# Graph recommender kernel: edges sorted into buckets that follow one another without padding, and a ring of 72 gathered tiles read through registers

## The reference: what is computed

```python
h = emb; acc = emb
for _ in range(2):
    h = jax.ops.segment_sum(adj_val[:, None] * h[adj_col], adj_row, num_segments=N)
    acc = acc + h
graph_item_embs = acc / 3
combined = graph_item_embs[items] + item_features[items]
seq_hidden = jnp.take_along_axis(combined, alias_inputs[..., None], axis=1)
... # masked mean, tanh, sigmoid gate, weighted sum over a session
item_out = _l2norm(graph_item_embs)      # scores = session vectors x all nodes
```

## Time and profile before

| what | value |
|---|---|
| median of 3 runs | 4148.01 us |
| the profiled execution | 4146.78 us, span 4145.0 us |
| mean granted TensorE clock | 0.755 of full |
| POOL busy | 2890.5 us (70%) |
| DVE busy | 3058.7 us (74%) |
| PE busy | 3105.1 us (75%) |
| layer 0, first to last gather | 742.7 to 2238.7 us |
| layer 1, first to last gather | 2265.7 to 3761.7 us |

### The profile page before, as it was taken

One profiled execution on the slowest core, in us unless ns is written; L12 is line 12 of the kernel. 1 busy time (PEld: TensorE's weight loads), 2 busy tenths in 40 slices (PEclk: granted clock), 3 DMA queues, 4 the chain that ended last, 5 costly groups with the idle time before them and its releaser, 6 DMA issues.

```text
span 4145.0 us, 77740 instructions
## 1 busy us (share of the span) xinstructions
PE 3105.1 (75%) x14462; PEld 2477.2 (60%) x14462; DVE 3058.7 (74%) x7236; ACT 824.8 (20%) x2833; POOL 2890.5 (70%) x2966
## 2 busy tenths in 40 slices
PE   4899998577777777777775777777777777776798
PEld 2777776466665666656664666666656665563454
DVE  8999997677777777777775676777767777677575
ACT  0899999000000000000000000000000000004553
POOL 2466766777777777777775777777777777775770
PEclk8899998676767777777766676777777777775898
DMA  1000000222222222222233222222222222233143
GB/s 36 3 4 3 3 3 3 57 55 55 55 55 55 55 55 55 55 55 55 55 100 119 56 56 55 55 56 55 56 55 56 55 55 56 55 116 102 58 155 144
DMA packets 156580, 236.68 MB, mean 57 GB/s; under 512 B 67566, under 2 KB 108216, under 8 KB 156184
## 3 DMA queue, kind: packets, MB, share of 16 engines
q0 software_dynamic: 92896, 171.14, 15.4%
q1 hardware_dynamic: 48364, 59.22, 4.2%
q10 hardware_dynamic: 15052, 3.83, 0.6%
HBM read 192.69 MB, written 41.33 MB: 56 GB/s over the span
## 4 chain that ended last, share of the span: by engine, by line
POOL 50%; issue 22%; DVE 10%; PE 9%; DMA 6%; ACT 2%; SPq 0%; DVEq 0%; ACTq 0%; POOLq 0%
POOL ring L577 48%; DMA ring<-in_L_rec_emb,cring 3%; PE bank L1479 2%; DMA ring<-table,cring 2%; PE bank L1420 2%; ACT big L647 2%; POOL ring L600 2%; DVE stage L926 1%; DVE big L870 1%; PE bank L1507 1%; DVE big L886 1%; DVE ring L1101 1%; DVE ring L878 1%; PE bank L1365 1%; PE bank L1466 1%
## 5 line engine op out<-in xcount | busy, mean ns | idle before, releaser
L1420 PE MATMUL bank<-ring 128*128 128x128 f32 x9952 | 2199.2, 381 | 816.2 <-DVE ring L1101 784.3
L1420 PEld LDWEIGHTS bank<-ring 128*128 128x128 f32 x9952 | 1831.2, 270 | 1184.0 <-DVE ring L1101 1158.4
L1101 DVE TENSOR_SCALAR ring<-bank,mlo,mval 128x256 f32<-128x256 f32 x2488 | 1349.2, 542 | 734.8 <-DMA ring<-table,cring 385.8
L577 POOL DMA_INDIRECT ring<-table,cring x1195 | 1132.4, 948 | 390.5 <-issue 355.9
L577 POOL DMA_INDIRECT ring<-in_L_rec_emb,cring x1195 | 1132.5, 948 | 368.8 <-issue 355.7
L1151 DVE TENSOR_TENSOR acc<-acc,bank 128x256 f32 x2488 | 1025.0, 412 | 142.5 <-issue 138.5
L663 ACT COPY mlo<-ring 128x24 f32 (+1 forms) x104 | 22.0, 211 | 2882.2 <-PE bank L1420 2793.3
L647 ACT ACTIVATE big<-big 128x68 f32<-128x68 bf16 x1764 | 557.3, 405 | 0.0
L1365 PE MATMUL bank<-big,ring 128*128 128x136 f32 x2352 | 441.5, 325 | 60.5 <-DVE ring L878 15.9
L545 POOL DMA_INDIRECT sorted_edges<-moved,block_to x313 | 399.9, 1278 | 101.7 <-issue 101.7
L1365 PEld LDWEIGHTS bank<-big,ring 128*128 128x128 f32 x2352 | 349.1, 212 | 150.9 <-ACT big L647 130.3
(11 more groups left out here) (210 smaller groups left out, 1438.7 us busy)
## 6 DMA issues: line engine op xcount, KB each, us to landing
ring<-in_L_rec_emb SPq DMA_DIRECT2D x3136, 0.5 KB
ring<-in_L_rec_emb ACTq DMA_DIRECT2D x3136, 0.5 KB
ring<-table SPq DMA_DIRECT2D x3136, 0.5 KB
ring<-table ACTq DMA_DIRECT2D x3136, 0.5 KB
scores<-stage SPq DMA_DIRECT2D x48, 512.0 KB, 2.7
ring<-in_L_rec_emb,cring POOLq DMA_INDIRECT x1195, 3.6
ring<-table,cring POOLq DMA_INDIRECT x1195, 3.5
table<-acc SPq DMA_DIRECT2D x7, 896.0 KB, 9.9
```

The costliest lines, as they stand in the source:

```text
L577: pool.indirect_dma_start(msg[:, s, :], None, source, bass.IndirectOffsetOnAxis(cring[:, s:s + 1], 0)).then_inc(s_g[s], 16)
L1101: dve.tensor_scalar(onehot[:, u % SR, :], bank[7][:, 0:BUCKET], mlo[:, u:u + 1], mval[:, u:u + 1], ALU.is_equal, ALU.mult).then_inc(s_S[u ...
L1420: last = pe.matmul(bank[u % PR][:, q * D:(q + 1) * D], onehot[:, u % SR, q * P:(q + 1) * P], msg[:, h * T + u, :], start=True, stop=True)
```

## The change

The bucket totals are no longer padded to tiles: a bucket starts where the one before ends (at a multiple of 4). That leaves GT = 1194 tiles of 128 slots per layer, but a tile may now hold edges of two buckets. The unit of the products becomes a *pass*: one tile and one bucket. There are 1194 + 48 passes, rounded up to 1244, so the number of products, `onehot` and adds is what the number of tiles was. A tile that crosses a border is gathered once and multiplied twice, each time with the values of the other bucket's edges set to zero.

- **Maps.** After the sort DVE computes for each bucket its first tile and first pass, PE turns these into per-pass tables (12 matmuls of 416 columns), and DVE derives which slots are valid in a pass, `pick` (a matrix that copies a tile's column to its passes), `slot_off` (the ring slot of a pass's tile, in elements) and `upto` (the group of gathers that a group of four passes needs). `m_lo` and `m_val` come from products with `pick` in place of transposes. The three matmuls for `tile_off` move from before the sort to after it.
- **Ring.** `msg` has RING = 72 slots in place of 48. PE reads the slot through a register; it loads 24 slot offsets and 6 group numbers per step.
- **Hand-over.** DVE no longer waits for gathers. POOL issues them in groups of four tiles; before group g it waits until group g - 2 has landed (for a group with an own tile, until its 128 one-row DMAs have, too) and raises `s_gd`; PE waits for `s_gd` against a register every four passes.
- **Pacing.** POOL's waits for products come only from tile 72 on: before tile 4g (g even) pass 4g - 16 must be done.
- **Own tiles.** 48 instead of 49 per layer, so POOL issues 1146 gathers per layer; the rows of own tile r start when the passes up to 24r are done (r = 1 and 2 need no wait on SP).
- The gather reads its indices from `m_col` directly; `cring` and its copy are gone.

```diff
+    GT = -(-(E + GR * NB * (R - 1)) // P)
+    NU = GT + NB - 1
-    NOWN = NST - 3
+    NOWN = GST - 2
+    RING = 3 * T
+    BEHIND = RING - (NB - 1)
+    GRP4 = 4
...
@@ sync
+            def own_tile(layer, source, r, h):
+                if not (isinstance(r, int) and r < 3):
+                    sp.wait_ge(s_mm[M - 1], r * (T // M) + PER * layer)
+                own_rows(source, r * HALF - HALF, h)
...
@@ gpsimd
+            def group_landed(layer, gi):
+                c, q = divmod(gi, T // GRP4)
+                pool.wait_ge(s_g[q], landed_of(layer, gi))
+                if is_own(T * c + GRP4 * q + GRP4 - 1):
+                    pool.wait_ge(s_line[c % 3], 16 * P)
+                    pool.sem_clear(s_line[c % 3])
+                pool.sem_inc(s_gd, 1)
+            def gather_group(layer, source, gi):
+                if gi >= 2:
+                    group_landed(layer, gi - 2)
+                if gi % 2 == 0 and GRP4 * gi >= RING:
+                    pool.wait_ge(s_mm[M - 1], PER * layer + (GRP4 * gi + 2 * GRP4 - BEHIND) // M)
+                for j in range(GRP4 * gi, min(GRP4 * gi + GRP4, GT)):
+                    if is_own(j):
                         continue
-                    if u % PACE == 0:
-                        done = NU * layer + T * c + u - AHEAD
-                        if done > 0:
-                            pool.wait_ge(s_mm[(done - 1) % M], (done - 1) // M + 1)
-                    pool.indirect_dma_start(msg[:, s, :], None, source,
-                                            bass.IndirectOffsetOnAxis(cring[:, s:s + 1], 0)).then_inc(s_g[s], 16)
+                    pool.indirect_dma_start(msg[:, j % RING, :], None, source,
+                                            bass.IndirectOffsetOnAxis(m_col[:, j:j + 1], 0)).then_inc(s_g[gi % (T // GRP4)], 16)
...
+                for gi in range(NGRP):
+                    if layer == 0 and gi == T // GRP4:
+                        pool.wait_ge(s_mrdy, 3)
+                    gather_group(layer, source, gi)
...
@@ scalar
-            act.wait_ge(s_toff, 3)
+            act.wait_ge(s_lcc, 1)
...
+            def round_rows(layer, source, r, k):
+                fetch(layer, r + 1, (k + 1) % 2)
+                own_rows(source, r * HALF - HALF, k % 3)
...
@@ vector
-            link(dve.tensor_scalar(toti[:, :], tot[:, :], float(P - 1), None, ALU.add))
-            link(dve.tensor_single_scalar(toti2[:, :], toti[:, :], P.bit_length() - 1, ALU.arith_shift_right))
-            link(dve.tensor_copy(ntile[:, :], toti2[:, :]))
...
-                if u % T < T - 1:
-                    dve.wait_ge(s_g[u], 16 * (FED[u] * layer + it + 1))
...
+                if u % T == 0:
+                    dve.wait_ge(s_mr, it * 2 + (NST * layer + u // T + 1))
...
@@ tensor
+                _, offs = nc.values_load_multi_w_load_instructions(
+                    slot_off[:, bass.ds(c * T, T)], engines=[mybir.EngineType.PE],
+                    min_val=0, max_val=(RING - 1) * D, skip_runtime_bounds_check_because=HERE)
+                _, need = nc.values_load_multi_w_load_instructions(
+                    upto[:, bass.ds(c * (T // M) + PER * layer, n // M)], engines=[mybir.EngineType.PE],
+                    min_val=1, max_val=LAYERS * NGRP)
+                for u in range(n):
+                    if u % M == 0:
+                        pe.wait_ge(s_gd, need[u // M])
                     pe.wait_ge(s_S[u % M], it * (2 * T // M) + (PER * layer + (T * h + u) // M + 1))
                     for q in range(2):
                         last = pe.matmul(bank[u % PR][:, q * D:(q + 1) * D], onehot[:, u % SR, q * P:(q + 1) * P],
-                                         msg[:, h * T + u, :], start=True, stop=True)
+                                         msg_flat[:, bass.ds(offs[u], D)], start=True, stop=True)
```

More of the change, by code:

```diff
@@ L110, in is_own, with landed_of @@
         return j % T == T - 1 and 1 <= j // T <= NOWN
-    FED = [sum(1 for j in range(u, NU, 2 * T) if not is_own(j)) for u in range(2 * T)]
-    assert T % 4 == 0 and max(TC[n + 1] - TC[n] for n in range(3)) <= 512
+    def landed_of(layer, gi):
+        c, q = divmod(gi, T // GRP4)
+        whole = [16 * sum(1 for k in range(GST) for j in range(T * k + GRP4 * q, min(T * k + GRP4 * q + GRP4, GT)) if not is_own(j))]
+        return layer * whole[0] + 16 * sum(1 for k in range(c + 1) for j in range(T * k + GRP4 * q, min(T * k + GRP4 * q + GRP4, GT))
+                                           if not is_own(j))
+    assert T % 4 == 0 and NP % 3 == 0 and NP // 3 <= 512 and NP - P * (NP // P) > 0 and P + NB - 1 <= 2 * P
+    HERE = "a pass's tile has its rows in one of RING slots: 0 to RING - 1, times D"
     with ExitStack() as ctx:
@@ L368, in recommender_program @@
         s_sid = sem("s_sid")
[L369 removed]
+        s_sq = [sem(f"s_sq{u}") for u in range(2 * NG)]
         s_x = sem("s_x")
@@ L448, in own_tiles @@
                     sp.wait_ge(s_t1w, 16 * (NB // GRP))
[L449 to L453, removed]
+                for r in range(1, 3):
+                    own_tile(layer, source, r, r)
+                with sp.Fori(1, NOWN // 3) as i:
+                    for h in range(3):
+                        own_tile(layer, source, 3 * i + h, h)
+                own_tile(layer, source, NOWN, 0)
             sp.wait_ge(s_mrdy, 3)
@@ new lines, in _ @@
+            some = plan[:, 4, :]
+            link(dve.tensor_copy(toti[:, :], start[:, :]))
+            link(dve.tensor_single_scalar(toti2[:, :], toti[:, :], P.bit_length() - 1, ALU.arith_shift_right))
+            link(dve.tensor_copy(ft, toti2[:, :]))
+            link(dve.tensor_scalar(toti[:, :], cum[:, :], float(P - 1), None, ALU.add))
+            link(dve.tensor_single_scalar(toti2[:, :], toti[:, :], P.bit_length() - 1, ALU.arith_shift_right))
+            link(dve.tensor_copy(le, toti2[:, :]))
@@ new lines, in _ @@
+            link(dve.tensor_tensor(le, le, ft, ALU.subtract))
+            link(dve.scalar_tensor_tensor(some, tot[:, :], 0.0, le, ALU.is_gt, ALU.mult))
+            link(dve.tensor_tensor_scan(begin, ones[:, 0:NB], some, 0.0, ALU.mult, ALU.add))
+            link(dve.tensor_tensor(begin, begin, some, ALU.subtract))
+            link(dve.tensor_tensor(shift, ft, begin, ALU.subtract))
+            dve.tensor_copy(bound[:, 2, :], shift)
+            link(dve.scalar_tensor_tensor(bound[:, 0, :], shift, -float(P), start[:, :], ALU.mult, ALU.add))
@@ new lines, in _ @@
+            link(dve.tensor_scalar(upto[:, 0:PER], upto[:, 0:PER], 1.0, None, ALU.add))
+            for n in range(3):
+                a, b = PC[n], PC[n + 1]
+                dve.wait_ge(s_map, n + 10)
+                last = dve.tensor_scalar(tile_off[0:1, a:b], bank[(3, 5, 6)[n]][0:1, 0:b - a], -1.0, float(BUCKET),
+                                         ALU.add, ALU.mult)
+            last.then_inc(s_slot, 1)
+            low_rows(0, 1, P).then_inc(s_low, 1)
+            for m in range(1, -(-NT // P)):
+                code_columns(m).then_inc(s_mtc, 1)
@@ new lines, in pass_chunk @@
+                last.then_inc(s_chk, 1)
+            pe.wait_ge(s_mapv, 9)
+            pe.wait_ge(s_meta0, 16)
+            turned(0)
+            pe.wait_ge(s_slot, 1)
+            pe.wait_ge(s_low, 1)
+            pass_chunk(0)
+            pe.wait_ge(s_meta, 32)
+            for m in range(1, -(-NT // P)):
+                turned(m)
+            pe.wait_ge(s_low, 3)
+            for m in range(1, -(-NP // P)):
+                pass_chunk(m)
+            pe.wait_ge(s_mta, -(-NP // P))
+            pe.wait_ge(s_pv, -(-NP // P))
```

286 lines of the change are left out of this document (185 added, 101 removed).

## The result

The changed kernel takes 4203.33 us (median of four runs, 4193.92 to 4204.8), the kernel before 4149.44 in the same set: a ratio of 1.013 (95% interval 1.0118 to 1.0143). The forecast was 4064 us, range 4028 to 4112, faster. It was wrong in sign and size.

A forecast was written before the change was run, and what follows sets the result against it. POOL's issue of gathers, 1.25 us each, was taken as the bound. Fewer gathers (-122.5) and smaller savings, less costs for landings, own rows, head and ends, summed to -83.3 us: 4064 us, range 4028 to 4112.

The forecast's parts named there:

- the wait for landed gathers: POOL's wait for group g-2: median landings cost nothing, only the late tail costs; +6 us over both layers, bounds 0 and 100.
- C: Rival: landing tails stop POOL in most steps, or later own-row rounds lose too; 52 us more, 4116 us; chance 0.13.
- forecast -122.5: Gathers on POOL: 1146 in place of 1195 a layer at 1.25 us each, -122.5 us over both layers.
- First gather: Start of layer 0's gathers: no wait for ACT's copy of `cring`, -0.8 us; start expected 2 us sooner, about 741.
- The head: First 24 gathers of layer 0: 7.5 us lost beside DVE operations, 4.3 before, and +1 us waiting for `m_col`.
- the 6 us more: Head of layer 0: if each DVE operation blocks POOL in full, about 6 us more, 4070 us in all.
- Own rows: POOL's wait for own tiles' row DMAs, mainly rounds 2 to 4: +16 us in layer 0, +12 in layer 1.
- PE: PE's step of 24 passes: 25.1 to 27.1 us with register loads of 2.2 to 4.2, under POOL's 27.6; nothing added.
- D: Rival: PE becomes the pace through step heads and address registers, 4240 us; decides from a 28.4 us step; chance 0.07.
- The increment: POOL's semaphore increment per group: taken as 0 us, running while the gather ahead is busy; otherwise 0.30 us each.
- rival E: The hand-over on POOL isn't hidden: 598 groups' increments of 0.30 us cost 179 us, 4243 us; chance 0.03.
- The ends of the layers: After each layer's last gather: hand-over by groups and a few more PE passes, +1.5 us a layer, +3 in all.

The follow-up runs named there:

- noown: Changed kernel without own tiles or their one-row DMAs, POOL gathering all 1194 tiles a layer: 4146.2 us, 0.9996 of the kernel before.
- lag5: Changed kernel with POOL waiting, before group g, for group g-5 in place of g-2: 4041.0 us, 0.974 of the kernel before.
- actrows: Changed kernel without SP's half of the own rows, 64 of 128 per tile, so part of the work is missing: 4031.0 us, 0.9717 of the kernel before.
- at16: Changed kernel with SP and ACT loading own-row offsets 16 at a time in place of 32, which spreads the rows out: 102 us off its time.

## Why the prediction was wrong

**The step that failed** is the wait for landed gathers: "Median landings cost nothing; the tail near 7.1 costs 0.9 to 2.1 us each time. I take **+6** over both layers". It cost about 160: the 185.7 us of excess less 16.7 at own rows, 6 in the first 24 gathers and the 3 or so that the kernel before has too. Of these 160, 144 end with the landing of a gather in the trace; the other 16 stand without a name. Two things are in it:

- The wait was priced too near. POOL starts 0.8 us after the landing that it waits for (median over 130 stalls), so landings must be in by 4.2 and 5.45 us, not 5 and 6.25. With the landings of the kernel before, by fours, that makes 11 us at the short waits and 5 at the long ones, 16 in place of 6.
- The landings were taken as given. They are a queue's, and the queue is shared with the own rows. With the landings measured in the changed kernel the same reckoning gives some 205 us if no stall moved the next; 160 was seen. The row of 2.3/3.6/7.1 held the warning: the median is half again the minimum, and in noown, without the rows, the same row reads 2.4/2.5/5.9. I read a tail as chance, where a plot over the gathers shows a sawtooth.

I had the mechanism as a rival (C, "the tail of the landings stops POOL in most steps") with 0.13, and priced it at +52; its real price is three times that. The bound of 100 us in the text was too low as well.

**The other terms held.** With the stalls gone, in lag5, layer 0 takes 1438.0 and layer 1 1431.5 us from first to last gather, together 122.6 us less than the earlier trace rows: forecast -122.5.
- First gather: 739.1 us, 3.6 earlier than before; forecast 1.8.
- The head: seven of the first 24 gathers took longer, 1.06 to 3.26 us; together they lost 6.2 us, forecast 8.5 with the wait for `m_col`. Each of the seven ended 0.12 to 0.22 us after a DVE operation of 0.68 us or more that reads and writes SBUF (the memory that holds the tiles), as the gather of 742.55 after L1208. Beside operations that read from the banks into which PE writes (L1189, L1195, L1217), and beside short ones, gathers took their 0.94 us.

```profile
742.55 2.01 POOL L627 DMA_INDIRECT ring<-in_L_rec_emb,ring  x1 [0.30 <-issue]
743.64 0.80 DVE L1208 TENSOR_SCALAR table<-table 1x1248 int32<-1x1248 f32 x1
744.87 0.95 POOL L627 DMA_INDIRECT ring<-in_L_rec_emb,ring  x1 [0.30 <-issue]
```

  The prediction charged a full block to each of DVE's operations, and the 6 us more did not come. The section of the Trainium skill that it names ("SBUF — State Buffer", "🔬 SBUF: two separate sides") gives the lock to some DVE operations only: those in a mode that uses both port pairs, and those with two inputs from SBUF against a GpSimd operation that reads SBUF. The seven gathers agree with such a lock; the over-reading was the prediction's.

- Own rows: 8.5 + 11.5 us, less 11 x 0.3 of ordinary gap, 16.7 us; forecast 28. The place was right (rounds 3 and 4 have 12.8 of it), but the third round of layer 0 lost 0.9 us, where I had 10.
- PE: no pace. The loads at a step's head cost more than my 4.2: 1.79 us for 24 values, 0.99 to 1.68 for 6 (median 1.65), and the register operations behind them, 5.5 us of its queue in the median of 104 steps (4.8 at the step below, from 1701.59 on). Products already queued covered a part, here more than half:

```profile
1700.69 3.77 PE L1598 MATMUL bank<-ring,shared 128*128 x16 [5.67 <-POOLq L616]
1706.57 6.57 PE L1598 MATMUL bank<-ring,shared 128*128 x32 [2.10 <-issue]
1713.40 2.05 PE L1598 MATMUL bank<-ring,shared 128*128 x16 [0.27 <-POOLq L616]
```

  Eight passes took 6.57 us, 0.82 each; 24 of them and 5.5 us make 25.2, under POOL's 27.6. With the prediction's own 0.96 a pass it would have been 28.4, the very step from which it said that D decides: that PE hid was closer than it reckoned. Rival D is out.
- The increment: noown has 598 of them and an excess of 10.4 us, of which 10.0 are longer gathers. It is hidden; rival E is out.
- The ends of the layers: +3.5 and +2.0 us, forecast +3. DVE's last adds, for the earlier trace rows:

```profile
2278.47 3.17 DVE L1290 TENSOR_TENSOR acc<-acc,bank 128x256 f32 x6
```

Sum by what was measured: -122.5 - 3.6 + 1.9 (head, 6.2 for 4.3) + 16.7 + 160 + 5.5 = +58, the difference of the two spans (4203.0 and 4145.0). The 160 is what the other terms leave over, so the sum closes by making; that it is landings is shown by the 144 us that end with one, and by noown, actrows and lag5.

**What stays open.** Why the landings are later in the changed kernel (4.65 us) than in the one before (3.4), though rows are issued at the same speed (22.6 us a round for SP in both) and gathers come no faster. A turn takes 1.56 us for 1.35, and about 1.4 in at16 and 1.5 in lag5, which doesn't follow the depth of the queue. A likely reading, argued only: at 8 rows in 1.35 us the path serves 5.9 rows a us of the 6.2 that SP and ACT issue, and the short pause in mid round lets it catch up; at 1.56 it serves 5.1, and the backlog outlasts the pause. What makes a turn longer was not found; the instruction packets are a small part.

## What to carry to other kernels

A landing time read from a trace belongs to the load that the trace has, and to a consumer that hardly looked at it. Before an in-order engine is made to wait for landings, look at their course over time, and ask which path the slowest of them shares, and with what: many small DMAs that all take one path delay a part of every large one. And give such a wait more distance than the landings measured so far, since they can move with it: here g-5 for g-2, one number, turned 1.3% slower into 2.6% faster, at the price of 12.6 us between the layers.

## What the runs showed that I had not expected

- 128 one-row DMAs of 512 B to 23 gathers make one path late, though DMA as a whole is busy for a quarter of the time (0.25 between 850 and 2240 us). At 64 rows nothing is late.
- Room feeds on itself: each group (5 us) of more distance raised the landings' median from 4.65 to 7.1, 11.6 and 15.1 us, and it paid each time all the same.
- Issue loops of 6 rounds (some 140 instructions a round and queue) show 141 packets of 8 KB on the instruction queue, loops of 2 rounds 14, in the same kernel and stretch. The likely reading is that the long ones are fetched anew in each turn.
- A gather beside a DVE operation on SBUF of 0.68 us or more ended 0.12 to 0.22 us after that operation, seven times in the first 24.
